# Heads 4 and 5 of samples 2 to 6 of each pair turned by DMA transposes as well

## The chip, the cores and the metric

The kernel runs on one core of a Trainium2 chip. The metric is the device time of one execution in microseconds, as the median of several runs.

## What is computed

The reference adds four layers to x of 8 samples x 128 tokens x 512 features, each with its residual: a gated MLP, two linear layers (all with low-rank adapters chosen per sample), and attention. The attention takes most of the time:

```python
q = rope(rmsnorm(x @ Wq)); k = rope(rmsnorm(x @ Wk)); v = x @ Wv     # 32 query heads, 8 key heads, D = 128
k_all = concat([cached_keys(512), k]); v_all = concat([cached_values(512), v])
scores = q @ k_all.T * SCALE, masked where the cache is not valid
o = softmax(scores) @ v_all                                           # 128 x 640 probabilities per head
x = x + o.reshape(...) @ Wo.T
```

## The kernel before, in words

Everything is float32. A number is split into a high part in the matmul format fp32r and the rest, and a product is three matmuls (high by high, high by low, low by high). For the probabilities this split has to be made of the transposed matrix: keys on the partitions, queries in the columns.

Attention runs over 4 pairs of key heads, and in each pair over the 8 samples; one unit is one pair and one sample, with 8 query heads in two groups of four (g = 0 and 1), 640 keys in JT = 5 blocks of 128. The 32 units go through a software pipeline, written by hand in `turn(pair, b, ...)` once per engine: the front half of turn n makes the queries, keys, scores and exponentials of unit n; its back half (u = n - 1) sums values by the probabilities of unit n - 1; the output product of unit n - 2 comes in between. `turns` (from line 1290) calls the turns of each pair: 0 and 1 written out, 2 to 6 as a hardware loop (`Fori`), 7 written out. Turns 7, 0 and 1 of pairs 0 to 2 also load and split the next pair's weights (`extra` is "next" or "out").

The order of work inside a turn is the order of the instructions on each engine; semaphores tie the engines together.

- TensorE, `turn` in `tensor_engine`: project the second queries, `output` (line 1729) of unit n - 2, wait for the turned probabilities (`s_tl`, line 1743), transpose four query heads (`transposes`, line 1645), sums of group 0 (`sums`, line 1662), and between them the transposes of group 1's probabilities into `wide[0]`, `wide[1]` (`probs_wide`, line 1656: 2 blocks x 4 heads each) and `bank[0]` (block 4 x 4 heads), the keys' and the second queries' transposes; then `values(1, 0)`, `values(1, 1)`, `values_new(1)`, the sums of group 1; then the eight `score(h)` (line 1692) with pieces of the next unit's projections between them.
- Group 0's probabilities (heads 0 to 3, tile `raw`) don't go through TensorE: GpSimd makes the first 2-byte part of two heads (`halve`, line 1393) and its rest (`make_rest`, line 1401, or VectorE's `rest_of` where GpSimd has weights to split), the SyncE queue turns each part with a DMA transpose (`turn_probs`, line 1552), and the turned parts become fp32r: the first on ScalarE (`high_turned`, line 1855), the rest on GpSimd (`low_turned`, line 1410, signals `s_tl`). k = 0, 1 counts the two-head parts, i = 0, 1 the first part and the rest.
- ScalarE copies group 1's transposed probabilities high (`high_probs`, line 1846, and line 1969), VectorE subtracts to get the low part (`low_probs`, line 2077, `low_new`, 2081).
- GpSimd in a turn: x load of the next sample (line 1317), `add_share` (store of y with accumulation, line 1372), `split_keys` (1351, 1353), weights' low parts if any (1360), `share_room` (1366, waits for that store), `split_values` (1381, 1386), `halve` twice, `low_turned` twice. `carry` (1343) is a tiny operation that takes the waits.
- SyncE in a turn, `load_unit`: 16 pages of keys of the next unit (1513), its rope table (1519), `turn_probs` of the current unit, 16 pages of values (1527). In turn 7 the queue, written out in `run`, holds weight chunks 0 to 7 of the next pair (1536) between `turn_probs` and the values, and 8 to 11 behind them. ScalarE needs these values in `high_values` (1869) ahead of its first exponential in that turn.

The inner turn waits for the rotated queries and keys of VectorE, `ra`, `qT`, `kT`; these are untouched. SBUF places are written by hand in `place` lines (1143 to 1179).

## Time and profile before

| | |
|---|---|
| Median of 3 runs | 1301.6 us (1297.05 to 1301.73) |
| The profiled execution | 1296.74 us, its span 1295.1 us |
| TensorE busy | 1277.9 us, 99% of the span, 6698 matmuls |
| VectorE, ScalarE, GpSimd busy | 935.0, 784.7, 768.0 us |
| Probability transposes on TensorE | 512 into wide, 128 into bank |
| DMA transposes | 128 |
| TensorE clock granted | 0.999 of full speed |

Busy time says how long an engine worked, not whether anything waited for it. The profile's chain of waits follows the work back from the end and so tells what had to be waited for. All times are of one profiled execution, counted from the start of its span.

### The profile page before, as it was taken

What the parts mean: (1) busy time and instruction counts of PE and PEld (TensorE: products, weight loads), DVE (VectorE), ACT (ScalarE), POOL (GpSimd) and SP (SyncE); (2) the same over time, 40 slices, a digit from 0 to 9 for tenths busy, and PEclk for the clock granted to TensorE, in tenths of its full rate; (3) what the DMA queues carried; (4) which work ended last, traced back from release to release, by engine and by line L of the source; (5) the groups of instructions that cost most, each with busy time, mean ns of one, the idle gap of its engine ahead of it and who ended that gap; (6) DMA issues with size and microseconds to landing.
All of it is one profiled execution on the core that took longest, in us unless ns stands there. A gap on an engine that the chain in (4) does not pass through costs nothing.

```text
span 1295.1 us, 26067 instructions
## 1 busy us (share of the span) xinstructions
PE 1277.9 (99%) x6698; PEld 1092.6 (84%) x6698; DVE 935.0 (72%) x2658; ACT 784.7 (61%) x1834; POOL 768.0 (59%) x792
## 2 busy tenths in 40 slices
PE   9999999999999999999999999999999999999998
PEld 8888877887888888888888888888888888888886
DVE  6532457778777777877777788777777977777774
ACT  6731334556666668676666676766656767656664
POOL 2110011348766668787666697866667869666663
PEclk9999999999999999999999999999999999999999
DMA  8321224176655558756555677655556775555543
GB/s 295 103 82 49 73 71 142 55 268 193 130 126 131 129 124 214 185 125 142 129 130 126 133 205 190 126 131 135 132 132 160 185 186 132 125 124 124 124 96 82
DMA packets 314896, 179.57 MB, mean 139 GB/s; under 512 B 260418, under 2 KB 279234, under 8 KB 314562
## 3 DMA queue, kind: packets, MB, share of 16 engines
q1 hardware_dynamic: 295840, 125.83, 40.8%
q0 software_dynamic: 12032, 35.40, 10.4%
q10 hardware_dynamic: 6946, 17.44, 4.4%
q8 instruction: 32, 0.52, 0.2%
q14 instruction: 46, 0.38, 0.1%
HBM read 119.71 MB, written 16.91 MB: 105 GB/s over the span
## 4 chain that ended last, share of the span: by engine, by line
PE 78%; SPq 7%; issue 5%; DVE 4%; POOL 2%; DMA 2%; ACT 1%; POOLq 0%; DVEq 0%; ACTq 0%
PE bank L1624 15%; PE tail L1662 13%; PE wide L1692 12%; PE tail L1729 10%; PE wide L464 4%; PE wide L1656 4%; PE wide L544 3%; PE bank L1645 3%; PE bank L464 3%; PE tail L464 3%; SPq L1513 2%; SPq L1527 2%; PE wide L599 2%; SPq L1552 2%; DMA turned<-parts 1%
## 5 line engine op out<-in xcount | busy, mean ns | idle before, releaser
L1662 PE MATMUL tail<-prT,vt 128*128 128x512 f32 x960 | 258.5, 409 | 0.7 <-POOL prT L1410 0.5
L1662 PEld LDWEIGHTS tail<-prT,vt 128*128 128x128 f32 x960 | 172.0, 190 | 40.4 <-DVE prT L2077 10.0
L1343 POOL TENSOR_TENSOR tick<-tick 128x1 f32<-128x1 f32 x254 | 57.9, 228 | 220.7 <-PE tail L1662 77.0
L1729 PE MATMUL tail<-woT,oT 128*128 128x512 f32 x768 | 179.5, 389 | 0.9 <-DVE oT L2129 0.9
L1729 PEld LDWEIGHTS tail<-woT,oT 128*128 128x128 f32 x768 | 144.0, 188 | 31.2 <-DVE oT L2129 1.3
L1692 PE MATMUL wide<-kT,qT 128*128 128x320 f32 x512 | 158.7, 310 | 1.8 <-DVE mx L2105 1.5
L1692 PE MATMUL wide<-kT_low,qT 128*128 128x320 f32 x512 | 158.2, 309 | 0.0
L1692 PE MATMUL wide<-kT,qT_low 128*128 128x320 f32 x512 | 157.9, 308 | 0.0
L1401 POOL TENSOR_TENSOR parts<-raw,parts 128x1280 f16<-128x1280 f32 x55 | 145.7, 2648 | 8.0
L1874 ACT ACTIVATE raw<-raw,nm,q_scale 128x640 f32<-128x640 f32 x124 | 114.6, 924 | 46.6 <-DVE nm L2108 45.0
L1874 ACT ACTIVATE pr<-pr,nm,q_scale 128x640 f32<-128x640 f32 x128 | 117.9, 921 | 35.7 <-DVE nm L2108 34.9
L2105 DVE CUSTOM_DVE_ANT_0 pr<-wide,bias 128x640 f32<-128x640 f32 x128 | 104.9, 820 | 40.7 <-issue 40.7
L2105 DVE CUSTOM_DVE_ANT_0 raw<-wide,bias 128x640 f32<-128x640 f32 x124 | 101.7, 820 | 15.9 <-issue 15.9
L1624 PE MATMUL bank<-wkvT,xTb 128*128 128x512 f32 x372 | 111.2, 393 | 0.0
L1692 PEld LDWEIGHTS wide<-kT,qT 128*128 128x128 f32 x512 | 96.1, 188 | 13.4 <-DVE mx L2105 1.8
L1624 PE MATMUL bank<-wq0T,xTb 128*128 128x512 f32 x372 | 106.1, 393 | 0.0
L1692 PEld LDWEIGHTS wide<-kT_low,qT 128*128 128x128 f32 x512 | 96.1, 188 | 10.2
L1855 ACT CAST prT<-turned 128x1280 fp32r<-128x1280 f16 x64 | 80.3, 1255 | 31.8 <-issue 27.8
L2077 DVE TENSOR_TENSOR prT<-wide,prT 128x1024 fp32r<-128x1024 f32 x64 | 78.2, 1224 | 27.7 <-ACT prT L1846 18.7
L1386 POOL TENSOR_TENSOR vt<-v_raw,vt 128x1280 fp32r<-128x1280 f32 x32 | 95.2, 2973 | 2.0
L1692 PEld LDWEIGHTS wide<-kT,qT_low 128*128 128x128 f32 x512 | 96.2, 188 | 0.0
L1624 PE MATMUL bank<-wq1T,xTb 128*128 128x512 f32 x372 | 89.4, 389 | 0.3 <-ACT bank L1832 0.3
(289 smaller groups left out, 2852.4 us busy)
## 6 DMA issues: line engine op xcount, KB each, us to landing
w_ring<-pair_weights SPq DMA_DIRECT2D x80, 256.0 KB, 3.9
k_raw<-k_pages SPq DMA_DIRECT2D x512, 32.0 KB, 1.7
v_raw<-v_pages SPq DMA_DIRECT2D x512, 32.0 KB, 2.8
spread<-one_over_denominators ACTq DMA_DIRECT2D x32, 512.0 KB, 4.8
xTb<-x_transposed POOLq DMA_DIRECT2D x31, 512.0 KB, 4.1
rope<-rope_tables SPq DMA_DIRECT2D x31, 256.0 KB, 2.7
out<-y POOLq DMA_DIRECT2D x31, 256.0 KB, 5.4
w_raw<-w_gate_up SPq DMA_DIRECT2D x10, 512.0 KB
```

The source lines that it names most:

```text
L464: last = nc.tensor.matmul(gate_up_place(j, c, w), wT[:, j % 2, w, w_part, k, :], x_half(x_part, k, c), start=(k == 0 and w_part + x_part = ...
L1343: nc.gpsimd.tensor_tensor(tick[:, 2:3], tick[:, 1:2], tick[:, 1:2], ALU.add).then_inc(s_carry, 1)
L1386: nc.gpsimd.tensor_tensor(vt[1][:, :, :], v_raw[:, :, :], vt[0][:, :, :], ALU.subtract).then_inc(s_vs, 1)
L1401: nc.gpsimd.tensor_tensor(dst[k][:, 1], src[:, k * HALF:(k + 1) * HALF, :], dst[k][:, 0], ALU.subtract).then_inc(s_rest[k], HALF)
L1624: last = nc.tensor.matmul(bank[i][:, :], x[:, x_part, k, :], w[:, w_part, k, :], start=(step == 0), stop=(step == NPROD - 1))
L1662: last = nc.tensor.matmul(tail[g][:, :], vt[v_part][:, j, g * D:(g + 1) * D], prT[p_part][:, :, j, :], start=(j == v_part == p_part == 0), ...
L1692: last = nc.tensor.matmul(out, (qT, qT_low)[q_part][:, g, i * S:(i + 1) * S], (kT, kT_low)[k_part][:, g, c * (NK // 2):(c + 1) * (NK // 2) ...
L1729: last = nc.tensor.matmul(place[:, :], oT[:, g, o_part, (h % REP) * S:(h % REP + 1) * S], woT[w_part][:, h, :], start=(h == o_part == w_pa ...
L1855: ac.copy(prT[0][:, k * HALF:(k + 1) * HALF].rearrange("p h j q -> p (h j) q"), turned[k][0]).then_inc(s_th[k], 1)
L1874: ac.activation(scores, scores, ACT.Exp, bias=nm[:, h:h + 1], scale=q_scale[:, 0, head(h)], accum_out=den[:, h:h + 1]).then_inc(s_exp, 1)
L2077: v.tensor_tensor(low, wide[w][:, :].rearrange("p (j h q) -> p j h q", j=2, h=REP), high_part, ALU.subtract).then_inc(t_free[w], 1)
L2105: v.tensor_tensor_reduce(halves(masked), scores, halves(bias[:, :]), 1.0, -3.0e38, ALU.add, ALU.max, mx[:, h:h + 1]).then_inc(s_sfree, 1)
```

## The change

Heads 4 and 5 (the first two of group 1) of samples 2 to 6 of every pair are no longer transposed by TensorE. GpSimd makes their two 2-byte parts in the buffer `parts[0]` once its first contents are turned, SyncE turns them into the place where their probabilities had been (`turned_third`), ScalarE and GpSimd turn them into fp32r in the next turn, in the place of heads 0 and 1 (`prT[...][:, 0:HALF]`) once group 0's sums have read it. Heads 6 and 7 stay as they were. The counters of `s_half`, `s_rest[0]`, `s_turned[0]`, `s_th[0]` and `s_tl` get the offset `before` (the count of third parts so far).

On TensorE, in turns 3 to 7, group 0's low sums are done in one piece before the second `probs_wide`; in group 1 all high sums come first, then all low ones. On SyncE the keys and values of the next unit are dealt out between the transposes; in turn 7's queue the two third transposes stand between weight chunks 4 and 5. Turn 2 is written out of the loop on all engines. `spread` waits for `turned[1][1]` instead of `turned[0][1]`.

```diff
-    pr = [place(135168 + h * 2560 if h < 6 else 163840 + (h - 6) * 2560, f"pr{h}", [P, NK]) for h in range(REP, HP)]
+    pr_third = place(145408, "pr_third", [P, HALF, NK])
+    pr = [pr_third[:, h, :] for h in range(HALF)] + [place(163840 + h * 2560, f"pr{REP + HALF + h}", [P, NK]) for h in range(HALF)]
+    turned_third = [place(145408 + i * 2560, f"turned_third{i}", [P, HALF * JT, S], F16)[:, :, :] for i in range(2)]
-    spread = place(135168, "spread", [P, G, REP * S])
+    spread = place(140288, "spread", [P, G, REP * S])
...
+    THIRDS = range(2, 7)
...
-            with eng.Fori(0, B - 3) as last:
-                turn(pair, last + 2, before(last + (pair * B + 2)), True, True, True, None, True, True)
+            turn(pair, 2, before(pair * B + 2), True, True, True, None, True, True)
+            with eng.Fori(0, len(THIRDS) - 1) as last:
+                turn(pair, last + 3, before(last + (pair * B + 3)), True, True, True, None, True, True)
...
+        def halve_third(u, before, n):
+
+            pool.wait_ge(s_exp, u * HP + 3 * HALF)
+            for i in range(2):
+                pool.wait_ge(s_turned[0][i], (u + before) * 16 + 16)
+            carry(n)
+            nc.gpsimd.tensor_copy(parts[0][:, 0], pr_third[:, :, :]).then_inc(s_half, 1)
+            pool.wait_ge(s_half, u * 2 + before + 3)
+            nc.gpsimd.tensor_tensor(parts[0][:, 1], pr_third[:, :, :], parts[0][:, 0], ALU.subtract).then_inc(s_rest[0], HALF)
+
+        def low_turned_third(u, before, n):
+
+            pool.wait_ge(s_turned[0][1], (u + before) * 16 + 32)
+            pool.wait_ge(s_pv, u * G + 1 + FIRST)
+            carry(n)
+            nc.gpsimd.tensor_copy(prT[1][:, 0:HALF].rearrange("p h j q -> p (h j) q"), turned_third[1]).then_inc(s_tl, 1)
...
                 split_keys(u, n)
                 n = n + 1
+            if has_third(b - 1):
+                low_turned_third(u - 1, thirds(pair, b - 1), n)
                 n = n + 1
...
+                halve(u, before, n + 2, 1, False, then_x is not None and extra != "next")
+                if has_third(b):
+                    halve_third(u, before, n + 3)
+                    n = n + 1
...
+        def turn_third(pair, b):
+
+            u, before = unit(pair, b), thirds(pair, b)
+            sp.wait_ge(s_rest[0], (u + before) * HALF + 2 * HALF)
+            for i in range(2):
+                sp.sem_inc(s_seen, 1)
+                sp.dma_start_transpose(turned_third[i], parts[0][:, i].rearrange("p h n -> p (h n)")).then_inc(s_turned[0][i], 16)
...
+            if has_third(b - 1):
+                load_rope(pair, b)
+                load_keys(pair, b, pages, 0, KEYS_FIRST)
+                turn_part(pair, b - 1, 0, 0)
+                load_keys(pair, b, pages, KEYS_FIRST, KEYS_FIRST + 2)
+                turn_part(pair, b - 1, 0, 1)
+                load_keys(pair, b, pages, KEYS_FIRST + 2, KEYS_FIRST + 4)
+                turn_part(pair, b - 1, 1, 0)
+                load_keys(pair, b, pages, KEYS_FIRST + 4)
+                turn_part(pair, b - 1, 1, 1)
+                load_values(pair, b, pages, 0, VALUES_FIRST)
+                turn_third(pair, b - 1)
+                load_values(pair, b, pages, VALUES_FIRST)
...
         KEYS_FIRST = 11
+        VALUES_FIRST = 4
+        WEIGHTS_FIRST = 5
...
-                turn_probs(unit(pair, B - 1) - 1)
-                load_weights(pair + 1, 0, NRING)
+                turn_probs(pair, B - 2)
+                load_weights(pair + 1, 0, WEIGHTS_FIRST)
+                turn_third(pair, B - 2)
+                load_weights(pair + 1, WEIGHTS_FIRST, NRING)
                 load_values(pair, B - 1, pages)
...
-                return [pr[i][:, j * P:(j + 1) * P] for i in range(REP)]
+                return [pr[i][:, j * P:(j + 1) * P] for i in range(HALF if third else 0, REP)]
...
-                if front:
+                if third:
+                    pe.wait_ge(s_rope, n * G + 2 + FIRST)
+                    transposes(0, [ra[:, REP + i, :] for i in range(G)])
+                    probs_wide(1, 0)
+                    sums(0, range(JT), (0,), 1).then_inc(s_pv, 1)
+                    probs_wide(1, 1)
+                elif front:
...
+            if third:
+                pe.wait_ge(s_yadd, u + FIRST)
+                pe.wait_ge(s_th[0], u + before_back + 2)
+                for w in range(2):
+                    pe.wait_ge(s_phi, u * 3 + w + 1)
+                    sums(1, (2 * w, 2 * w + 1), (0, 1), 0)
+                pe.wait_ge(s_phi, u * 3 + 3)
+                sums(1, (JT - 1,), (0, 1), 0)
+                for w in range(2):
+                    pe.wait_ge(t_free[w], u + 1 + FIRST)
+                pe.wait_ge(s_tl, u * 2 + before_back + 3)
+                sums(1, range(JT - 1), (0,), 1)
+                begin(0)
+                sums(1, (JT - 1,), (0,), 1).then_inc(s_pv, 1)
+            elif back:
...
+            def high_turned_third():
+
+                act.wait_ge(s_turned[0][0], (u + before_back) * 16 + 32)
+                ac.copy(prT[0][:, 0:HALF].rearrange("p h j q -> p (h j) q"), turned_third[0]).then_inc(s_th[0], 1)
...
-                act.wait_ge(s_turned[0][1], u * 16 + 16)
+                act.wait_ge(s_turned[1][1], u * 16 + 16)
...
+            if third:
+                high_turned_third()
             if back:
                 high_probs(0)
+            if third:
+                high_probs(1)
...
-                if not front:
+                if not front or third:
                     dve.wait_ge(s_pv, u * G + 1 + FIRST)
...
             if back:
                 low_probs(0)
+            if third:
+                low_probs(1)
             if front:
                 low(3, 1, qT_low[:, 1, :], bank[1][:, :], qT[:, 1, :])
```

## Rows read from the trace of the kernel before

**Rows 1.** The page, busy us, share of the span, instructions, by engine.
```profile
PE 1277.9 (99%) x6698; PEld 1092.6 (84%) x6698; DVE 935.0 (72%) x2658; ACT 784.7 (61%) x1834; POOL 768.0 (59%) x792
```

**Rows 2.** The chain of waits, inner turn, pair 0 to 1: start us, us, what.
```profile
653.82 0.44 PE bank L1645 x4
654.26 2.75 PE tail L1662 x12
657.01 0.87 PE wide L1656 x8
...
660.54 3.61 PE tail L1662 x15
664.16 0.88 PE wide L1692 x6
...
684.91 0.44 PE bank L1645 x4
```

**Rows 3.** Timeline of ScalarE, the same turn: start, us, engine, line, operation [idle before].
```profile
658.14 0.37 ACT L1840 CAST kT<-bank 128x256 fp32r<-128x256 f32 x1 [2.99 <-PE bank L1645]
658.41 1.02 ACT L1846 CAST prT<-wide 128x1024 fp32r<-128x1024 f32 x1
```

**Rows 4.** Timeline of GpSimd, the same turn.
```profile
655.30 0.89 POOL L1372 DMA_DIRECT2D out<-y  x1 [0.44 <-issue]
...
657.47 2.38 POOL L1353 TENSOR_TENSOR kT_low<-k_raw,kT 128x1024 fp32r<-128x1024 f32 x1
...
664.32 0.20 POOL L1343 TENSOR_TENSOR tick<-tick 128x1 f32<-128x1 f32 x1 [4.24 <-PE tail L1662]
...
669.14 1.25 POOL L1393 CAST parts<-raw 128x1280 f16<-128x1280 f32 x1
...
677.40 1.26 POOL L1410 CAST prT<-turned 128x1280 fp32r<-128x1280 f16 x1
681.01 0.19 POOL L1343 TENSOR_TENSOR tick<-tick 128x1 f32<-128x1 f32 x1 [2.36 <-DMA turned<-parts]
```

**Rows 5.** Timeline of the SyncE queue, the same turn.
```profile
660.09 9.13 SPq L1513 DMA_DIRECT2D k_raw<-k_pages  x16
...
670.48 8.29 SPq L1552 DMA_TRANSPOSE turned<-parts  x4
678.88 7.74 SPq L1527 DMA_DIRECT2D v_raw<-v_pages  x16
```

**Rows 6.** DMA transposes of line 1552, 600 to 740 us: ns min/median/max; landing.
```profile
L1552 SPq DMA_TRANSPOSE turned<-parts x20: 1255/1352/2190, 609.0 to 739.6; - x20
...
DMA to landing us min/median/max: 3.3/3.5/4.8
```

**Rows 7.** Landing of the values (L1527) first, of the y store (L1372) second.
```profile
DMA to landing us min/median/max: 1.6/2.8/6.8
...
DMA to landing us min/median/max: 4.1/5.4/9.0
```

**Rows 8.** Timeline of the SyncE queue where the next weights are loaded, pairs 0, 2.
```profile
494.87 8.22 SPq L1527 DMA_DIRECT2D v_raw<-v_pages  x16
...
998.38 9.30 SPq L1527 DMA_DIRECT2D v_raw<-v_pages  x16
```

**Rows 9.** ScalarE copies the values in turn 7, pairs 0 and 2.
```profile
508.14 1.27 ACT L1869 CAST vt<-v_raw 128x1280 fp32r<-128x1280 f32 x1 [0.92 <-DMA v_raw<-v_pages]
...
1010.50 1.27 ACT L1869 CAST vt<-v_raw 128x1280 fp32r<-128x1280 f32 x1
```

**Rows 10.** Query transposes of TensorE: starts of turns 7 and 0, pairs 0 and 2.
```profile
495.73 0.60 PE L1645 MATMUL bank<-ident,ra 128*128 128x128 f32 x4
...
527.97 0.66 PE L1645 MATMUL bank<-ident,ra 128*128 128x128 f32 x4 [1.00 <-POOL prT L1410]
...
998.80 0.60 PE L1645 MATMUL bank<-ident,ra 128*128 128x128 f32 x4
...
1030.55 0.66 PE L1645 MATMUL bank<-ident,ra 128*128 128x128 f32 x4 [0.51 <-POOL prT L1410]
```

More of the change, by code:

```diff
@@ L1414, in turn @@
             u = unit(pair, b)
+            before = thirds(pair, b)
             own = chunk_pair(pair, extra)
@@ L1462, in turn @@
                 split_values(u, n, not extra)
-                halve(u, n + 1, 0, False, extra != "next")
-                halve(u, n + 2, 1, False, then_x is not None and extra != "next")
+                halve(u, before, n + 1, 0, False, extra != "next")
+                halve(u, before, n + 2, 1, False, then_x is not None and extra != "next")
+                if has_third(b):
+                    halve_third(u, before, n + 3)
+                    n = n + 1
                 if extra == "next":
@@ L1469, in turn @@
                     low_weights(own, 4 * KT + 2, NCHUNK)
[L1470 to L1471 removed]
+            low_turned(u, before, n + 3, 0)
+            low_turned(u, before, n + 4, 1)
             if first_turn:
@@ L1520, in load_rope, with load_values @@
                          rope_scratch[bass.ds(b, 1)].rearrange("o p n -> (o p) n")).then_inc(s_ropel, 16)
-        def load_values(pair, b, pages):
+        def load_values(pair, b, pages, first=0, end=NPP):
             sp.wait_ge(s_vs, unit(pair, b) + FIRST)
-            for j, page in enumerate(pages):
+            for j in range(first, end):
+                page = pages[j]
                 i = j % (P // PSIZE)
@@ L1554, in load_unit, with turn_probs @@
+        def turn_third(pair, b):
+            u, before = unit(pair, b), thirds(pair, b)
+            sp.wait_ge(s_rest[0], (u + before) * HALF + 2 * HALF)
+            for i in range(2):
+                sp.sem_inc(s_seen, 1)
+                sp.dma_start_transpose(turned_third[i], parts[0][:, i].rearrange("p h n -> p (h n)")).then_inc(s_turned[0][i], 16)
+        def turn_probs(pair, b):
+            for k, i in ((0, 0), (0, 1), (1, 0), (1, 1)):
+                turn_part(pair, b, k, i)
         def load_unit(site, pair, b):
@@ L1577, in run @@
                 load_keys(pair + 1, 0, pages, 0, KEYS_FIRST)
-                turn_probs(unit(pair, B - 1))
+                turn_probs(pair, B - 1)
                 load_keys(pair + 1, 0, pages, KEYS_FIRST)
@@ L1585, in run @@
                 load_keys(pair + 1, 1, pages, 0, KEYS_FIRST)
-                turn_probs(unit(pair + 1, 0))
+                turn_probs(pair + 1, 0)
                 load_keys(pair + 1, 1, pages, KEYS_FIRST)
                 load_values(pair + 1, 1, pages)
-            with sp.Fori(0, B - 2) as b:
-                load_unit(5, NPAIR - 1, b + 2)
-            turn_probs(NPAIR * B - 1)
+            load_unit(8, NPAIR - 1, 2)
+            with sp.Fori(0, len(THIRDS)) as b:
+                load_unit(5, NPAIR - 1, b + 3)
+            turn_probs(NPAIR - 1, B - 1)
             sp.wait_ge(s_wlo, chunks_done(NPAIR, 0))
@@ L1608, in begin @@
                 pe.wait_ge(c_free[i], full[i].value() + FIRST)
+            before_back, third = thirds(pair, b - 1), back and has_third(b - 1)
             first_turn = isinstance(b, int) and b == 0
@@ L1748, in turn @@
             if back:
-                for k in range(2):
-                    pe.wait_ge(s_th[k], u + 1)
+                pe.wait_ge(s_th[0], u + before_back + 1)
+                pe.wait_ge(s_th[1], u + 1)
                 pe.wait_ge(s_vs, u + 1 + FIRST)
@@ L1764, in turn @@
                     rest.fourth_quarter()
-                pe.wait_ge(s_rope, n * G + 2 + FIRST)
-                transposes(0, [ra[:, REP + i, :] for i in range(G)])
-            if back and front:
+                if not third:
+                    pe.wait_ge(s_rope, n * G + 2 + FIRST)
+                    transposes(0, [ra[:, REP + i, :] for i in range(G)])
+            if back and front and not third:
                 sums(0, (2, 3), (0,), 1)
@@ L1818, in turn @@
             full0 = Count(c_full[0], before[0])
+            before_front, before_back, third = thirds(pair, b), thirds(pair, b - 1), back and has_third(b - 1)
+            first_head = HALF if third else 0
+            heads_there = REP - first_head
             def arrive():
@@ L1966, in turn @@
             if back:
-                high_probs(1)
+                if not third:
+                    high_probs(1)
                 act.wait_ge(c_full[0], before[0] + (4 if front else 1))
-                ac.copy(prT[0][:, :, JT - 1, :], bank[0][:, :].rearrange("p (h q) -> p h q", h=REP)).then_inc(s_phi, 1)
+                ac.copy(prT[0][:, first_head:, JT - 1, :], bank[0][:, 0:heads_there * S].rearrange("p (h q) -> p h q", h=heads_there)).then_inc(s_phi, 1)
                 early(3)
@@ L2016, in turn @@
             n, u = unit(pair, b), unit(pair, b - 1)
+            before_front, third = thirds(pair, b), back and has_third(b - 1)
+            first_head = HALF if third else 0
+            heads_there = REP - first_head
             full1 = Count(c_full[1], before[1])
@@ L2172, in turn @@
             if back:
-                low_probs(1)
+                if not third:
+                    low_probs(1)
                 low_new()
```

133 lines of the change are left out of this document (73 added, 60 removed).

## The prediction

> **What bounds the kernel now.** I read the busy table first: TensorE (PE) is busy in 99% of the span [rows 1], so time leaves this kernel only where PE gets less to do, and comes in where something makes PE wait. The chain of waits over an inner turn shows what one turn is made of [rows 2]. I count from T, the start of the four query transposes. From T = 653.82 to 684.91 is 31.09 us, all of it PE. A transpose of 128x128 costs 0.87/8 = 0.109 us there, a 512-column matmul 2.75/12 = 0.229 us. From T to the first score (664.16) there are 30 transposes and 30 matmuls, 3.27 + 6.87 = 10.14 us of work in 10.34 us, so about 0.2 us is waiting inside. All other engines must merely be in time. Next come their timelines in that turn: ScalarE idles 2.99 us before the new keys [rows 3]; GpSimd idles 4.24 us before the values of the unit and 2.36 us for the last DMA transposes [rows 4]; the SyncE queue issues 16 keys in 9.13 us, four transposes in 8.29 with waits between them, and 16 values in 7.74 [rows 5].
>
> **The parts of the change.** There are 20 units with the third transposed part (samples 2 to 6 of four pairs), felt by PE one turn later, in turns 3 to 7 of each pair.
>
> PE: heads 4 and 5 no longer pass through it: 2 heads x 5 blocks = 10 transposes less, 1.09 us a turn. The new order (all of group 0's sums, then all high sums of group 1, then all low ones) puts the low sums 2.3 us behind the high ones, so the 0.2 us of waiting should go too: 1.29 us a turn, T to first score 9.05 us, turn 29.8 us.
>
> ScalarE and VectorE: the high copies of wide probabilities (1.02 us of 1024 columns, [rows 3]) halve and one 1280-column cast comes in, some 1.3 us at that rate; it stands behind the new keys' copy, now at T+3, in time in which ScalarE idled [rows 3]. Group 1's first sums are due at T+5.6, the cast ends by T+4.6 and the first half-wide copy about 0.6 later, estimated as half of 1.02 with a start. VectorE's subtractions halve and now wait for group 0; queued behind them are the second queries' low part, the mask and the first normalisation, which end near T+8.7 before the first score is complete near T+9.9. Cost 0; cover gone, it would be at most the 0.2 us I counted as won.
>
> GpSimd: one halving with its rest comes in, 4.13 us (two took 677.40 - 669.14 = 8.26, [rows 4]), and one cast with its carry, 1.4 us. The cast stands behind the split of the keys (ends 657.47 + 2.38, T+6.0), so it ends at T+7.5, before PE wants it at T+7.9: it lies in the idle 4.24 us. The halving lies on GpSimd's chain: resumed at T+10.5 before, T+9.2 now; the two halvings end at T+22.3, the third at T+26.4, the two casts at T+29.1, and PE waits for the second at T+29.8. Slack 0.7 us, where it was 2.5. The old wait of 2.36 us for a transpose is what makes the place. The third halving also waits for the second transpose: its source is ready at T+18.1, it lands 3.5 us after issue in the median, 4.8 at most [rows 6], so at 21.7 against 22.2, or 0.7 late at most, which the slack takes.
>
> SyncE: two transposes more, 1.35 us each by their median pitch [rows 6], 2.7 us. In inner turns they stand between 4 and 12 of the values' transfers, the first issued at T+26.5 when the third rest is ready. The 12 values (0.48 us each) are then issued until T'+5.2, T' being the next T, and before until about T'+1.7. The last one lands 2.8 us after its issue in the median, 6.8 at most [rows 7]: near T'+7.7, wanted at T'+9.2. The keys' queue starts at T+6.2, waiting for GpSimd, as before. Hidden, with 1.5 us to spare. These bursts also meet the x load, the spread of shares and the store of y; the store holds GpSimd before the value split. It is issued at 655.30 (T+1.5) and lands 5.4 us later in the median, 9.0 at most [rows 7].
>
> The Trainium skill, Advanced Engine Details and Errata, section X-Bar Transpose (TRN2), holds transposes to be as fast as regular DMAs, 350 to 400 GB/s. A part is 128x1280x2 bytes, so this trace's pitch is 243 GB/s and it disagrees; by the page two would take an estimated 1.9 us, and the sum below would come out near -17 us.
>
> The turn that loads the next pair's weights (turn 7, pairs 0 to 2): here SyncE has no room. Eight weight chunks are issued and then 16 values, issued until 503.09 in pair 0 (T'+7.4, T' = 495.73) and 1007.68 in pair 2 (T'+8.9, T' = 998.80) [rows 8, 10]. ScalarE copies these values high before its first exponential: at T'+12.4 in pair 0, after waiting 0.92 us for the landing, and at T'+11.7 in pair 2 [rows 9]. From that copy to the next turn's query transposes it is 19.83 and 20.05 us, and PE waited 1.00 and 0.51 us for GpSimd's last cast at the end [rows 10]. So in this turn a chain is the bound: values, exponentials, halving, rests, weight splits, casts, PE. The two third transposes now stand among the eight chunks ahead of all 16 values: issue ends 2.7 us later. Landing becomes T'+15.1 in pair 0 and 14.2 in pair 2, while ScalarE would be ready at about T'+10.3. Added: 2.7 and 2.5 us, in pair 1 between 1.8 and 2.7. The saving at PE is swallowed, since PE waits anyway. Bounds: -1.29 a turn if the values aren't late, and +4.0 if the third rest is late as well and holds the queue. I take 2.4, from the two rows, times 3 = +7.2 us.
>
> Turn 2 of each pair is written out instead of looped: the trace shows nothing that this costs by itself; bounds -0.2 and +1 us a pair, taken as 0.
>
> **Sum.** 17 turns (3 to 6 of four pairs, and 7 of the last) x -1.29 = -21.9; three turns x +2.4 = +7.2; together -14.7 us. The profiled execution took 1296.74 us (span 1295.1), so 1282.0. It lies 4.9 us under the median of the runs, 1301.6, which becomes 1286.9. I say 1286.
>
> **Rivals.**
> Everything hidden: the values of turn 7 land in time because the DMA engines had drained by then. Pair 2's landing within 2.8 us of the last issue speaks for it, pair 0's 5 us against. Then turn 7 gains between 0 and 1.29: -21.9 to -25.8, some 1278.
>
> GpSimd's chain becomes the bound: its slack of 0.7 us is used up in inner turns. If the store of y lands at its slowest, T+10.5 instead of T+9.2, 1.3 us less 0.7 of slack is lost, leaving 0.7 of the saving: 16 x 0.7 + 1.3 saved, 7.2 lost, 5.3 us faster, 1296. For: the values are pushed into just that stretch. Against: the median landing leaves 2.3 us.
>
> Slower: the values queue behind the third transposes and land too late in every inner turn. It decides from a landing at T'+11.2 (9.2 + 0.7 slack + 1.29). At the slowest landing of the rows, 6.8 us, they come at T'+11.6, costing 0.4 a turn net: 16 x 0.4 - 1.3 + 7.2 = +12, some 1314. For: a queue in order, with two transposes ahead. Against: median 2.8 us.
>
> That the change wouldn't do what it says is excluded by counting below; the diff slices the heads in each step.
>
> **From these to the numbers.** Chances: forecast 0.50, everything hidden 0.14, GpSimd's chain 0.24, slower 0.12. A measurement of this kernel tells about 0.5% from no change, 6.5 us: 1295.1 and 1308.1 are the limits. The first two are faster, the third mostly (its shallower forms) and the rest of it within, the slower case mostly slower: 0.78, 0.12, 0.10. The forecast's own range is 1281 to 1292 (turn 7 between +0 and +4, inner turns 1.1 to 1.3). With the hidden case and most of the third it is 1276 to 1298, which leaves out the slower case and the tails.
>
> **What would show it.** Transposes into wide fall from 512 to 352, those of pr into bank from 128 to 88. Inner turns go from 31.1 to 29.8 us with no PE wait for GpSimd's cast; GpSimd's wait for turned goes from 2.36 to near 0. In turn 7 ScalarE waits 3 to 5 us for v_raw, and PE waits longer than 1.0 us at its end (3 to 5). It would be wrong if inner turns stay above 30.5, which is the GpSimd case if its wait is for out or turned, the slower one if it is for v_raw; or if turn 7 is no longer than 32.2, which is the hidden case.

## The result, and the profile after

The changed kernel takes 1328.0 us (median of four runs, 1317.8 to 1344.8) against 1300.8 before: ratio 1.019, interval 1.012 to 1.026. It is slower by 27 us, where 1286 was forecast. One of its four runs, the longest, was a disturbed one and is not in the ratio. The profiled execution took 1324.7 us.

The chain's shares before:

```profile
PE 78%; SPq 7%; issue 5%; DVE 4%; POOL 2%; DMA 2%; ACT 1%; POOLq 0%; DVEq 0%; ACTq 0%
```

From the page of the changed kernel: the busy table, SyncE's DMA queue (packets, MB, share of the engines), the chain's shares, and landings (count, KB each, median us).

```profile
PE 1269.7 (96%) x6498; PEld 1079.0 (82%) x6498; DVE 907.9 (69%) x2658; ACT 788.2 (60%) x1854; POOL 874.0 (66%) x892
...
q1 hardware_dynamic: 348320, 138.95, 47.1%
...
PE 35%; SPq 28%; issue 14%; POOL 8%; DMA 6%; DVE 4%; ACT 4%; POOLq 0%; DVEq 0%; ACTq 0%
...
v_raw<-v_pages SPq DMA_DIRECT2D x512, 32.0 KB, 4.2
...
xTb<-x_transposed POOLq DMA_DIRECT2D x31, 512.0 KB, 7.1
...
out<-y POOLq DMA_DIRECT2D x31, 256.0 KB, 7.6
```

PE was busy in 99% of the span [rows 1] and is at 96% now. It has its 200 instructions less (6498 for 6698). Of the chain it holds 35%, where it was 78%, and SyncE's own queue 28%, where it was 7%. The values, 2.8 us to landing before, need 4.2 in the median, the store of y 7.6 for 5.4 [rows 7]. That is the outline of a kernel whose arithmetic got shorter and whose transfers bound it more than before.

The same answer comes from one inner turn taken whole, with the windows view (busy us of each engine in the stretch, then granted clock, DMA share, GB/s). The kernel before, from T to T':

```profile
653.82:684.91 31.09, 31.09 (x170) 26.98 (x169) 23.85 (x75) 19.39 (x49) 20.65 (x21) 1.00 0.56 127
```

The changed kernel, the same turn:

```profile
664.54:695.85 31.31, 30.29 (x159) 25.85 (x159) 20.97 (x70) 18.89 (x49) 26.09 (x27) 1.00 0.70 148
```

The turn has less for PE and yet is longer, and PE is idle in about a microsecond of it. GpSimd has 5.4 us more, as the sum said.

Summed over the profiled executions, turn by turn: the sixteen inner turns (3 to 6 of four pairs) take 505.8 us for 497.3, turn 7 of pairs 0 to 2 takes 39.4, 39.4 and 34.1 for 32.2, 32.3 and 31.8 (together +16.7), and everything else between turn 1 and the last +2.8. That is the 28 us. One inner turn of the sixteen lasted 38.0 us. In it the second third transpose landed 12.0 us after its issue, PE waited 5.12 us for GpSimd's cast of it, and then ran at a mean granted clock of 0.52, that is nearly all the time at 1.2 GHz instead of 2.4. The late transposes thus cost more than the wait itself. The wait, and the window behind it:

```profile
907.17 2.50 PE L1744 MATMUL tail<-prT,vt 128*128 128x512 f32 x5 [5.12 <-POOL prT L1433]
906.00:912.00 6.00, 4.83 (x14) 4.27 (x15) 0.68 (x2) 0.00 (x0) 3.36 (x5) 0.52 0.43 95
```

What the engines wait for, from the waits view of the changed kernel (total us, times, longest):

```profile
POOL tick L1358 <- DMA turned_third<-parts: 29.6, 12, 5.8
POOL tick L1358 <- DMA v_raw<-v_pages: 27.4, 16, 2.7
PE bank L1727 <- POOL prT L1442: 19.2, 16, 2.3
...
PE tail L1744 <- POOL prT L1433: 17.7, 8, 5.1
```

GpSimd waits for the new transposes and for the values, PE for GpSimd. But the decisive view is that of SyncE's own queue. Here is one round of it in the changed kernel (start, us, what; a gap between two rows is the queue's own, as no wait is shown in it):

```profile
660.37 1.99 SPq L1574 DMA_DIRECT2D v_raw<-v_pages  x4
662.54 3.27 SPq L1608 DMA_TRANSPOSE turned_third<-parts  x2
665.92 6.76 SPq L1574 DMA_DIRECT2D v_raw<-v_pages  x12
674.45 0.36 SPq L1565 DMA_DIRECT2D rope<-rope_tables  x1
675.13 6.45 SPq L1559 DMA_DIRECT2D k_raw<-k_pages  x11
681.90 1.37 SPq L1600 DMA_TRANSPOSE turned<-parts  x1
683.54 1.06 SPq L1559 DMA_DIRECT2D k_raw<-k_pages  x2
684.82 1.36 SPq L1600 DMA_TRANSPOSE turned<-parts  x1
686.45 1.03 SPq L1559 DMA_DIRECT2D k_raw<-k_pages  x2
687.85 1.34 SPq L1600 DMA_TRANSPOSE turned<-parts  x1
689.45 0.42 SPq L1559 DMA_DIRECT2D k_raw<-k_pages  x1
690.09 1.26 SPq L1600 DMA_TRANSPOSE turned<-parts  x1
691.44 2.12 SPq L1574 DMA_DIRECT2D v_raw<-v_pages  x4
```

From 660.37 to 691.44 is 31.07 us. 26.67 of it is issuing, 1.77 lies ahead of the rope table (where the queue closes its loop and reads sixteen page numbers), and 2.6 in eleven gaps of 0.1 to 0.4 us. Nothing is left. Without the third transposes this round is 31.07 - 3.27 = 27.8 us: I take that as what SyncE needs in any case, and 29.8 was to be the new turn. Two rows tell the same in one line each. Before, SyncE stood waiting for its key buffer:

```profile
SPq L1513 <- POOL kT_low L1353: 49.6, 20, 3.1
```

and in the changed kernel it is hardly ever there in time to wait:

```profile
SPq L1559 <- POOL kT_low L1368: 4.8, 4, 2.8
```

### The profile page after: what moved, and what is told of

The parts are those of the page before. It is cut to its first block, busy times and chain, and to the rows that moved or that the text cites. A ratio compares the mean times of both kernels' runs of the same rounds, so it can differ in the third digit from the quotient of the medians.

```text
span 1323.1 us, 25871 instructions
## 1 busy us (share of the span) xinstructions
PE 1269.7 (96%) x6498; PEld 1079.0 (82%) x6498; DVE 907.9 (69%) x2658; ACT 788.2 (60%) x1854; POOL 874.0 (66%) x892
## 3 DMA queue, kind: packets, MB, share of 16 engines
q1 hardware_dynamic: 348320, 138.95, 47.1%
## 4 chain that ended last, share of the span: by engine, by line
PE 35%; SPq 28%; issue 14%; POOL 8%; DMA 6%; DVE 4%; ACT 4%; POOLq 0%; DVEq 0%; ACTq 0%
SPq L1574 9%; SPq L1559 8%; SPq L1600 7%; PE tail L1744 4%; PE wide L464 4%; PE bank L1706 4%; PE wide L544 3%; SPq L1608 3%; PE wide L1774 3%; DMA v_raw<-v_pages 3%; DMA turned<-parts 3%; PE tail L1811 2%; PE bank L464 2%; PE tail L464 2%; PE wide L599 2%
## 5 line engine op out<-in xcount | busy, mean ns | idle before, releaser
L1744 PEld LDWEIGHTS tail<-prT,vt 128*128 128x128 f32 x960 | 176.8, 194 | 62.6 <-issue 14.4
L1358 POOL TENSOR_TENSOR tick<-tick 128x1 f32<-128x1 f32 x294 | 66.0, 225 | 134.0 <-DMA turned_third<-parts 29.6
L405 POOL DMA_INDIRECT b_rows<-b,row_pair x8 | 8.8, 1106 | 116.7 <-DVE act_hl L878 114.9
L2198 DVE TENSOR_TENSOR prT<-wide,prT 128x512 fp32r<-128x512 f32 (+1 forms) x64 | 55.0, 887 | 44.2 <-ACT prT L1953 35.6
L1706 PEld LDWEIGHTS bank<-wq1T,xTb 128*128 128x128 f32 x372 | 69.7, 188 | 15.9 <-issue 0.7
```

The source lines that it names most:

```text
L1706: last = nc.tensor.matmul(bank[i][:, :], x[:, x_part, k, :], w[:, w_part, k, :], start=(step == 0), stop=(step == NPROD - 1))
L1744: last = nc.tensor.matmul(tail[g][:, :], vt[v_part][:, j, g * D:(g + 1) * D], prT[p_part][:, :, j, :], start=(j == v_part == p_part == 0), ...
```

## The theories

**B, SyncE's time.** The queue issues in order and each issue takes time, also where nothing waits. The new transposes fill what room it had, the keys, transposes and values behind them come late each turn, and the delay goes round. This took its sharp form only after the fifth and sixth run.

**A, the landing.** The new transposes go out when the load of x, the spread of the shares, the store of y and in turn 7 the weight chunks go out; all of them share the DMA engines, so the transposes and what is queued behind land late.

**C, GpSimd.** Its 4.13 us of halving and a cast more use up the 0.7 us of slack.

## The experiments

All are edits of the changed kernel. In e1, e2, e5, e6 and e9 the probabilities of heads 4 and 5 are not transposed (they are copied, or read as they are), so their part of the output is another; all the rest runs as before.

### e1: no third transposes

```diff
-                sp.dma_start_transpose(turned_third[i], parts[0][:, i].rearrange("p h n -> p (h n)")).then_inc(s_turned[0][i], 16)
+                sp.sem_inc(s_turned[0][i], 16)
```

The casts read the untransposed part.

> Leaves out the 40 third DMA transposes: ScalarE and GpSimd cast the untransposed parts instead, so the probabilities of heads 4 and 5 are wrong; all other work of the change stays (TensorE's 200 transposes less, GpSimd's third halving and cast). Theory A (the third transposes meet the x load, the spread of shares, the store of y and the weight chunks in the DMA engines at the start of the next turn, land late and hold TensorE and the values): without them the inner turns take about 29.8 us and turn 7 at most 32.3, together 1270 to 1283 us. Theory C (GpSimd's added 5.5 us a turn are the bound): inner turns stay at 31 us, the whole above 1295 us.

1285.6 us, ratio 0.989 (0.987 to 0.991). Fifteen of the sixteen inner turns take 29.81 to 30.00 us, twelve of them 29.81 to 29.84. With all of GpSimd's new work in place this is the forecast turn to 0.03 us: C falls for the inner turns, PE's term of the sum stands. Turn 7 is 33.8 us all the same, where theory A had at most 32.3. That is 1.5 to 2.0 above before, so part of its loss has nothing to do with the transposes. It isn't the values either: ScalarE copies them 10.9 to 11.5 us into this turn, sooner than before (11.7 to 12.4). GpSimd, which also has the third cast in this turn, is busy in 30.4 of its 33.8 us (28.7 of 32.1 before, both in the mean of three), and PE waits for it, first for that cast and then for the last one:

```profile
PE bank L1727 <- POOL prT L1442: 7.9, 7, 2.0
PE tail L1744 <- POOL prT L1433: 3.8, 3, 1.3
```

So C keeps a part of turn 7.

### e2: copies in four pieces

```diff
-                sp.dma_start_transpose(turned_third[i], parts[0][:, i].rearrange("p h n -> p (h n)")).then_inc(s_turned[0][i], 16)
+                for c in range(4):
+                    n0 = slice(c * 32, (c + 1) * 32)
+                    sp.dma_start(turned_third[i][n0].rearrange("p j q -> p (j q)"), parts[0][n0, i].rearrange("p h n -> p (h n)")).then_inc(s_turned[0][i], 16)
```

> In place of each third transpose four plain DMA copies of the same bytes inside SBUF, at the same place in the SyncE queue; their issue takes about as long (8 x 0.35 = 2.8 us beside 2 x 1.4), and the probabilities of heads 4 and 5 are not transposed, so wrong. Theory A (what the transposes cost in the DMA engines counts): near e1, 1272 to 1288 us, landing of the copies about 2 us. Theory B (the 2.7 us of issue ahead of the values count, in turn 7 above all): turn 7 stays at 36 us or more and the whole stays above 1300 us.

1347.5 us, ratio 1.036 (1.034 to 1.038): far from A's 1272 to 1288, and above the 1300 that B had named, though turn 7 took 34.7 to 37.5 us and not always 36. The eight copies took SyncE 0.59 us each, 4.7 in all for 2.8, and landed late themselves (4.7 us in the median), so the run changed two things at once and sized neither. Read later, it is the first point for B: a round of 27.8 + 4.7 = 32.5 us, and inner turns of 33.3 in the mean.

### e3: without sample 6

```diff
-    THIRDS = range(2, 7)
+    THIRDS = range(2, 6)
```

> Samples 2 to 5 only: no third part in turn 6, so none among the weight chunks; TensorE transposes four heads again in turn 7. By theory A turn 7 goes back from 39.4, 39.4 and 34.1 us to 32.3 each, so about 16 us come back, 1308 us; the inner turns keep their disturbance. If the loss of turn 7 only moves to another turn (the queue is late anyway), the time stays within 5 us of the changed kernel's, 1320 to 1330.

1316.2 us (1310.8 to 1325.0), ratio 1.013 (1.009 to 1.018). Turn 7 is back at 31.4 to 32.4 us. The inner turns were worse in this execution, 32.6 us in the mean with six of 33.6 to 39, though the edit touches only turn 6 of them (no third halving there, and it is written out). All six are like the one of 38.0 in the changed kernel: PE waits 1.9 to 5.7 us for GpSimd's third cast, and the granted clock of the turn then falls to 0.90 to 0.95. Such turns come and go from one execution to the next. PE's wait for the third cast in e3:

```profile
PE tail L1748 <- POOL prT L1434: 22.1, 7, 5.7
```

### e4: spread and x later

```diff
             if back:
-                spread_shares()
...
                 high(1, 2, qT[:, 0, :], bank[1][:, :])
+                if third:
+                    spread_shares()
```

and GpSimd's load of x behind its store of y.

> The changed kernel with the transfers that meet the third transposes issued later in turns 3 to 7: the spread of shares behind ScalarE's copy of the first queries (some 0.8 to 3 us later), the x load behind the store of y (2.5 us later). Theory A: the third transposes land nearer 3.5 us after issue than 5.5 and inner turns shorten by up to 1 us, 1295 to 1315 us. Theory B or C: no change, 1320 to 1330 us; slower if the spread then comes late for the normalisation.

1310.7 us, ratio 1.008 (1.006 to 1.011). GpSimd's wait for the third transposes falls from 29.6 to 0.8 us. What A says of their landing is true. The landing of those transposes, changed kernel (min, median, max), and then e4:

```profile
DMA to landing us min/median/max: 3.4/5.5/13.8
```

```profile
L1616 SPq DMA_TRANSPOSE turned_third<-parts x40: 1252/1413/3060, 369.4 to 1262.2; - x40
...
DMA to landing us min/median/max: 3.4/3.5/7.6
```

Turn 7 comes to 34.1, 34.8 and 35.1 us, from 39.4, 39.4 and 34.1. But only 17 of the 42 us between the changed kernel and e1 came back, 9 of them in turn 7, and the wait moved. In e4:

```profile
L1358 POOL TENSOR_TENSOR tick<-tick 128x1 f32<-128x1 f32 x294 | 68.5, 233 | 130.9 <-DMA v_raw<-v_pages 61.8
```

61.8 us of waiting for values, where it had been 27.4. Late landing was not all.

### e5 and e6: small copies, whole copies

In e5 four copies of 128 partitions by 64 bytes stand for each transpose:

```diff
-                sp.dma_start_transpose(turned_third[i], parts[0][:, i].rearrange("p h n -> p (h n)")).then_inc(s_turned[0][i], 16)
+                for c in range(4):
+                    sp.dma_start(turned_third[i][:, 0, c * 32:(c + 1) * 32], parts[0][:, i, 0, c * 32:(c + 1) * 32]).then_inc(s_turned[0][i], 16)
```

and in e6 one copy of its 320 KB:

```diff
-                sp.dma_start_transpose(turned_third[i], parts[0][:, i].rearrange("p h n -> p (h n)")).then_inc(s_turned[0][i], 16)
+                sp.dma_start(turned_third[i].rearrange("p j q -> p (j q)"), parts[0][:, i].rearrange("p h n -> p (h n)")).then_inc(s_turned[0][i], 16)
```

> In place of each of the two third transposes four copies of 128 partitions by 64 bytes: eight DMAs that move 64 KB together instead of 640 KB, and take SyncE some 0.5 to 0.6 us each by the run of plain copies, 4.7 us in all against 2.8 for the two transposes. Casts read the untransposed part. Theory A (the DMA engines are overfull while the third transposes run): the bytes are gone, inner turns come to about 29.9 us and the run to 1284 to 1293 us. Theory B (what is queued ahead of the twelve values on SyncE delays them by its issue time): the values are issued 1.9 us later than in the changed kernel, and the run is not faster than 1328, about 1328 to 1345 us.

> In place of each third transpose one plain copy of the same 320 KB, from SBUF to SBUF, 128 partitions by 2560 bytes; SyncE is busy with each for about 0.6 us instead of 1.4. Theory A, if it is the bytes: the engines are as full as in the changed kernel and the run stays within 1315 to 1335 us; if it is what a transpose does to the engines, about 1290 to 1305 us. Theory B: the values are issued 1.6 us earlier than in the changed kernel, most of the loss goes, 1285 to 1300 us.

e5: 1337.4 us, ratio 1.028 (1.025 to 1.030). A tenth of the bytes, and slower than the changed kernel. e6: 1285.7 us, ratio 0.989 (0.986 to 0.991). All of the bytes, and every inner turn and turn 7 within 0.3 us of e1's. The third copies of e6:

```profile
L1608 SPq DMA_DIRECT2D turned_third<-parts x40: 490/508/560, 369.3 to 1235.9; - x40
...
DMA to landing us min/median/max: 2.4/2.7/5.5
```

and one of its inner turns, all PE, with the engines moving more bytes in less of their time than in the changed kernel (154 GB/s at a share of 0.63, there 148 at 0.70):

```profile
650.04:679.87 29.83, 29.83 (x159) 25.99 (x159) 22.43 (x74) 19.47 (x50) 25.98 (x27) 1.00 0.63 154
```

So the bytes cost nothing, while 4.8 us in SyncE's queue instead of 1.0 to 1.15 cost 52 us a run. That is strong support for B, if not a clean measure of it: e5 also has 160 transfers for 40, and they land in 4.3 us in the median. Since a transpose takes 1.4 us and a whole copy 0.5, e6 leaves open whether the transposes hurt by their time in the queue or by what they do in the engines.

### e7 and e8: the order of the queue

```diff
-                load_keys(pair, b, pages, 0, KEYS_FIRST)
+                load_keys(pair, b, pages)
                 turn_part(pair, b - 1, 0, 0)
-                load_keys(pair, b, pages, KEYS_FIRST, KEYS_FIRST + 2)
+                load_values(pair, b, pages, 0, 2)
                 turn_part(pair, b - 1, 0, 1)
...
```

e8 is this, the edit of e4 and the edit of e3.

> The changed kernel with SyncE's order alone changed: a turn's sixteen keys go out together, and five of the sixteen values between the transposes of the turn, so that eleven DMAs instead of sixteen lie behind the third transposes and the last values go out about 2 us earlier. Theory A: the third transposes still meet the loads of the turn's start, GpSimd's and TensorE's waits for them (29.6 us and 17.7 us in all) stay, those for v_raw (27.4 us) go: 1300 to 1318 us. Theory B: values no longer late, 1285 to 1298 us.

> Both cures together and without the third halving in sample 6: the order of e7_values_first, the spread transfers and the load of x of the next turn issued after the third transposes instead of beside them, third transposes for samples 2 to 5 alone. Theory A: neither the third transposes nor the values are late, inner turns 29.9 to 30.3 us, turn 7 as before: 1281 to 1292 us, faster than both kernels. Theory B says the same of the values but gives the later loads no part: then no faster than e7_values_first by more than 5 us. If both miss a cost that lies in GpSimd's longer chain, it stays above 1300 us.

e7: 1321.3 us, ratio 1.017 (1.014 to 1.021), a miss for both. e8: 1296.3 us, ratio 0.997 (0.995 to 0.999), also above what was expected. In e7 GpSimd waits 10.6 us for values instead of 27.4, but still 23.0 for the third transposes and 26.6 for the ordinary ones (26.0 in the changed kernel). In e8, set against e4, its wait for values falls from 61.8 to 35.5 us, and the one for the ordinary transposes rises from 27.2 to 45.2. An order moves a full queue's lateness from one transfer to another; it takes nothing out of the round. In e8 the third transposes land in 3.5 us (5.5 at most) and SyncE has few waits left, so what keeps its inner turns at 30.7 us should be SyncE's time; that is argued.

### e9: nothing transposed, the same time in the queue

e6 and three small copies behind the two whole ones (which leave those 96 columns out).

```diff
+            for c in range(3):
+                sp.dma_start(to[:, c * 32:(c + 1) * 32], part[:, c * 32:(c + 1) * 32]).then_inc(s_turned[0][1], 16)
```

> Whole plain copies as in e6_whole_copies, and three small copies of 128 partitions by 64 bytes behind them, so that SyncE is again busy for about 2.8 us (2 x 0.5 and 3 x 0.6) in the place of the two third transposes, with nothing transposed and the same bytes. Theory B, now with its number: SyncE needs about 28.3 us of issuing in each inner turn beside the third transposes, so a turn is as long as 28.3 us and what stands in their place, if that is over TensorE's 29.8: inner turns of 31.1 us and about 1303 to 1315 us. Theory A (what a transpose does in the DMA engines delays the other transfers): inner turns of 29.8 to 30.1 us, 1284 to 1292 us.

1303.7 us, ratio 1.005 (1.002 to 1.007), inner turns of 30.9 us in the mean. The expectation had 28.3 + 2.8 = 31.1; with what stands in the queue it is 27.8 + 3.07 = 30.9, B's number. The round of e9's queue shows what was put in (1.15 and 1.92 us):

```profile
684.70 2.06 SPq L1574 DMA_DIRECT2D v_raw<-v_pages  x4
686.95 1.15 SPq L1609 DMA_DIRECT2D turned_third<-parts  x2
688.14 1.92 SPq L1611 DMA_DIRECT2D turned_third<-parts  x3
690.18 6.13 SPq L1574 DMA_DIRECT2D v_raw<-v_pages  x12
```

Set against each other, with the round taken as 27.8 us and what stands in the third transposes' place:

| kernel | in their place, us | 27.8 + that | mean inner turn |
|---|---|---|---|
| e1 | 0 | 27.8 | 29.89 |
| e6 | 1.15 | 28.95 | 29.93 |
| e9 | 3.07 | 30.9 | 30.89 |
| e2 | 4.7 | 32.5 | 33.29 |
| e5 | 4.8 | 32.6 | 33.05 |
| changed | 2.8 to 3.3 | 30.6 to 31.1 | 31.62 |

Up to PE's 29.8 us SyncE's work is free; beyond it each microsecond in the queue is about one in the turn. e2 and e5 lie 0.8 and 0.5 us above that line. The mean granted clock of their inner turns is 0.981 and 0.990 (1.00 in e1, e6 and e9), by which they lost an estimated 0.6 and 0.3 us a turn, so most of the excess is the clock's.

18 us lie between e6 and e9. But 24 more lie between e9 and the changed kernel, whose queue holds about the same time. These I give to A, by difference; the changed kernel's own runs spread over 14 us, so the figure is rough. Between the two profiled executions it is 21.6 us: 10.9 in turn 7, where e9 has 33.9 to 34.1 us and the changed kernel 39.4, 39.4 and 34.1, and 11.6 in the inner turns, 7.2 of it the one of 38.0.

Turn 7 of pair 1, the changed kernel's SyncE queue (T' = 759.22):

```profile
756.32 5.43 SPq L1608 DMA_TRANSPOSE turned_third<-parts  x2
762.01 1.99 SPq L1583 DMA_DIRECT2D w_ring<-pair_weights  x3
764.10 8.48 SPq L1574 DMA_DIRECT2D v_raw<-v_pages  x16
```

The two transposes hold the queue for 5.43 us instead of 2.7, five weight chunks being ahead of them. The windows behind them in the changed kernel (granted clock, DMA share and GB/s at the end):

```profile
760.00:765.00 5.00, 5.00 (x21) 4.02 (x21) 1.12 (x2) 2.00 (x4) 4.92 (x7) 0.71 1.27 137
```

and in e9 at the same distance from T' (752.18):

```profile
753.00:758.00 5.00, 5.00 (x32) 4.31 (x31) 1.60 (x3) 4.11 (x8) 4.92 (x7) 1.00 1.09 366
```

The engines are full in both; with transposes in flight they deliver 137 GB/s, in e9 366. The two stretches don't hold quite the same transfers, as e9's whole copies have landed by then. The granted clock of 0.71 is a mean: PE, which had waited 2.20 us at 759.22, ran a part of this stretch at 1.2 GHz instead of 2.4. The values are then issued until T'+13.4, and ScalarE copies them at T'+20.4 (e9: T'+12.7):

```profile
779.61 1.27 ACT L1982 CAST vt<-v_raw 128x1280 fp32r<-128x1280 f32 x1 [2.75 <-issue]
```

### e10 and e11: the third transposes from ScalarE

```diff
+            def turn_third(i):
+                act.wait_ge(s_rest[0], (u + before_back) * HALF + 2 * HALF)
+                act.wait_ge(s_turned[1][1], u * 16 + 16)
+                act.sem_inc(s_seen, 1)
+                act.dma_start_transpose(turned_third[i], parts[0][:, i].rearrange("p h n -> p (h n)")).then_inc(s_turned[0][i], 16)
...
+            if third:
+                turn_third(0)
             if share and not shares_first:
                 copy_share()
             if back:
                 spread_shares()
+            if third:
+                turn_third(1)
```

SyncE waits for their landing before its next transpose. e11 is this without sample 6.

> The changed kernel with the two third transposes issued by ScalarE, one before and one behind its copy of y and its spread transfer, and nothing of them on SyncE; the same crossbar work and bytes at nearly the same place of the turn. Theory B (SyncE's issue time is the bound): inner turns of 29.8 to 30.4 us, turn 7 of pairs 0 to 2 about 34 us, 1284 to 1297 us. Theory A: the third transposes still meet the other transfers and land late; inner turns stay above 31 us, 1310 to 1330 us.

> e10_from_scalar with the third halving in samples 2 to 5 alone. Turn 7 of pairs 0 to 2 goes back to about 32 us and one inner turn of the last pair to 31.1. Theory B: 1280 to 1291 us, about 4 us under e10_from_scalar and the fastest correct kernel so far. Theory A: 1305 to 1325 us.

1443.3 us, ratio 1.111 (1.107 to 1.116), and 1406.6 us, ratio 1.082 (1.078 to 1.085): far outside what either theory had. SyncE was relieved, but the transposes stood alone in another queue while SyncE issued sixteen values. ScalarE issues them, and GpSimd has them 10 us later:

```profile
702.23 1.39 ACTq L2009 DMA_TRANSPOSE turned_third<-parts  x1
...
705.28 1.96 ACTq L2009 DMA_TRANSPOSE turned_third<-parts  x1
```

```profile
715.70 0.19 POOL L1358 TENSOR_TENSOR tick<-tick 128x1 f32<-128x1 f32 x1 [5.13 <-DMA turned_third<-parts]
```

```profile
DMA to landing us min/median/max: 3.5/9.8/17.8
```

9.8 us to landing in the median, 17.8 at most, 135.3 us of waiting on GpSimd. PE waits 88.1 us for the third cast, and the mean granted clock of the run is 0.948, where it was 0.990 in the changed kernel. This is theory A at its strongest: here a transpose that shares the engines with other queues' transfers lands late. SyncE's ordinary transposes, issued between the keys later in the turn, kept 3.4 to 3.5 us in the median in every run.

### e12 to e14: four values from ScalarE

```diff
+            def first_values():
+                held = [act.alloc_register(f"value_page{turn_no[0]}_{j}") for j in range(4)]
+                act.load(held, table[0:1, bass.ds(b, 1), 0:4].rearrange("p b j -> p (b j)"))
...
+                for j in range(4):
+                    act.dma_start(v_raw[j * PSIZE:(j + 1) * PSIZE, 0, :],
+                                  v_pages[bass.ds(pages[j] * NPAIR + pair, 1)].rearrange("o s n -> (o s) n")).then_inc(s_v, 16)
...
-                load_values(pair, b, pages, 0, VALUES_FIRST)
```

e13 is this without sample 6, e14 is e13 with e4's edit.

> The changed kernel with the first four values of the turns that have third transposes issued by ScalarE at the turn's start instead of SyncE: SyncE has 2.2 us less to issue, some 26.1 us beside the third transposes' 2.8, so 28.9 in all. If SyncE's issue time is about half of the loss and the third transposes' late landing the other half (as e6 and e9 against the changed kernel say): inner turns of 30.0 to 30.6 us, turn 7 still above 36, 1298 to 1312 us. If SyncE's time is all of it: 1285 to 1296 us. If it is the late landing alone: 1318 to 1332 us.

> e12 with the third halving in samples 2 to 5 alone, so that no third transpose stands in turn 7. Both halves: turn 7 at 32 us, inner turns as in e12, 1286 to 1300 us. SyncE's time alone: 1280 to 1290. Late landing alone: 1308 to 1320.

> e13 with ScalarE's spread transfer and GpSimd's load of x issued behind the places where they meet the third transposes, as in e4. Both halves: nothing of either is left, inner turns of 29.8 to 30.2 us, 1279 to 1289 us, faster than both kernels. If the four values on ScalarE's queue meet the ordinary transposes instead, or x comes late for TensorE's projections, it stays above 1290 us.

e12: 1311.0 us, ratio 1.009 (1.006 to 1.013). 17 us come back by taking four short issues from SyncE; e6 and e9 had given 18 for that part. The inner turns fall from 31.6 to 30.7 us, turn 7 stays at 37.6, 36.2 and 34.4. e13: 1290.5 us, ratio 0.993 (0.991 to 0.996): turn 7 at 32.2 to 32.8, inner turns of 30.3 in the mean, seven of the sixteen within 0.25 us of PE's 29.8. The two causes add up as expected, and this version is faster than both kernels, by 0.7% than the one before. Its values are copied at T'+12.6 to T'+14.0 in turn 7, later than in e1, and yet the turn is 1.0 to 1.6 us shorter than there: it has no third cast.

e14: 1303.9 us, ratio 1.003 (1.001 to 1.005), a miss. With SyncE in time moving the load of x later no longer helps the third transposes: they land in 3.7 us in the median (5.3 at most), for 4.0 (5.8) in e13. The last wait is now PE's for GpSimd's cast of the third part. e14 and then e13:

```profile
PE tail L1755 <- POOL prT L1434: 17.8, 14, 1.8
```

```profile
PE tail L1747 <- POOL prT L1434: 1.3, 3, 0.5
```

Why GpSimd is late there (the load of x now stands behind the store of y in its order) was not tried apart.

## Why the prediction was wrong

**PE's term, right.** 1.29 us a turn was forecast; e1 and e6 give 31.08 - 29.83 = 1.25. The transposes into wide are 256 + 96 = 352, those of pr into bank 64 + 24 = 88, as counted.

**GpSimd, right for inner turns.** "Slack 0.7 us, where it was 2.5" held: in e1 its longer chain costs nothing.

**SyncE, the step that failed.** "The keys' queue starts at T+6.2, waiting for GpSimd, as before. Hidden, with 1.5 us to spare." The keys start at 675.13, T+10.6 (T = 664.54), and wait for nobody. The step laid each burst beside its own consumer and never summed the queue over a turn. The rows had most of it: 9.13 + 8.29 + 7.74 us were shown [rows 5], of which the 8.29 held waits, and two transposes of 1.35 us make it 27.9. A whole round is 26.7 us of issuing and 4.4 us of gaps, most of which the rows don't show: 31.1 us, more than the 29.8 that the same text gave the turn. The values are issued until T'+8.1 in the round shown (672.68; T' = 664.54), not T'+5.2. The turn gets back none of PE's 1.29.

**The landing, a second term of the same step.** 3.5 us in the median and 4.8 at most were carried over from transposes that go out alone [rows 6] to a place where two other queues, ScalarE's and GpSimd's, are active; that the bursts meet was said, and priced at nothing. Measured there: 5.5 and 13.8. For the values 2.8 and 6.8 became 4.2 and 10.0.

**Turn 7, a term mis-sized and a term left out.** +2.4 each was forecast, upper bound +4.0; it was +7.1, +7.2 and +2.4. The +2.4 of pair 2 is luck in part: there the copy came 0.9 us later than forecast and the rest took 1.0 less. The chain was read rightly (from the values' copy to the next query transposes 19.0 to 20.3 us, for 19.83 and 20.05 forecast), but the landing at T'+14 to 15 became T'+19.0, 20.4 and 15.1 in the three pairs. The values do queue behind the transposes, but these held the queue 5.43 us in pair 1 for 2.7 where weight chunks are in flight. The term left out is GpSimd's third cast, priced for the inner turns only. Without the transposes turn 7 is still 1.5 to 2.0 us longer (e1), and e6 and e9 are within 0.4 us of e1, though the values are copied at T'+12.7 to T'+14.3. In e3 and e13, without a third part in this turn, it is 31.4 to 32.8 us. No run takes out the cast alone.

**The sum.** Forecast: inner turns -20.6 (16 turns), turn 7 +7.2, the last turn -1.3. Measured: +8.5, +16.7 and -0.5, and +2.8 in all other turns, 0.6 of it in turn 2, which was taken as 0. Of the 42 us between the changed kernel and e1, 18 are SyncE's time (e6 to e9) and 24, by difference, the transposes' way through the engines (e9 to the changed kernel), with the lower clock behind PE's waits in it. e12, which takes away mostly the first cause, gives back 17, and e4, which takes away mostly the second, 17 as well.

**The rivals.** The slower one, values behind the third transposes in every inner turn, is nearest to what happened: GpSimd waits for values 16 times, 27.4 us in all (6.4 before). Its price of 0.4 us a turn came from the landing alone, and it got 0.12. The doubt set against it, the median landing of 2.8 us, was a figure of the kernel whose queue still had room. What the Trainium skill, Advanced Engine Details and Errata, X-Bar Transpose (TRN2), says of transposes, that they are as fast as regular DMAs, is contradicted further: 1.4 us of SyncE's time for 0.5 with the same 320 KB (e6), and 3.5 us to landing [rows 6] for 2.7. The forecast did use the measured 1.35 us; what failed was to add it up over the turn.

## What to carry to other kernels

Add up what each issuing queue does over one whole turn, with the gaps between issues and the loop's own overhead, and compare it with the turn that the change is to reach: a queue is an engine with a throughput, and the busy table does not list it. A duration to landing belongs to a place and to its neighbours in time; carried to a place where other queues are active, its maximum is the first guess and not its median. When a queue is full, fewer or shorter issues help; another order only passed the lateness on here (e8).

## What the hardware did that was not expected

A DMA transpose of 128x1280 two-byte elements takes 1.4 us of the issuing queue, a plain copy of the same bytes 0.5, a copy of 8 KB 0.6. By the packets of the queue (295840 before, 348320 after), each transpose adds 52480 / 40 = 1312 packets for 320 KB, some 250 bytes each; e6 adds 144 per copy. While other queues are active it lands in 5.5 us in the median instead of 3.5, and issued from ScalarE's queue beside SyncE's values in 9.8. A whole copy in its place lands in 2.7 (e6), but the quarter copies of e2 need 4.7 and the small ones of e5 4.3. That small packets take turns with the larger ones of other queues would explain it: a transfer cut into 1312 pieces would wait at more of them than one cut into 144. This is argued from the counts and was not tried by itself, and it can't be all: the copies of e2 have only 48 packets each. The Trainium skill, DMA: Bandwidth & Descriptors, section Queues, rings and completion order, says that each DMA engine takes turns between the queues that have work for it, a packet at a time; e10 against the changed kernel agrees with it in direction (9.8 us for 5.5), no run here shows the turns themselves, nor whether the packets that the profile counts are the ones meant there. When a transpose meets full engines, it also holds its queue: 5.43 us for two in turn 7, and 5.2 us for a single one at the most.
